# RWKV time mix of a two-layer decoder: logs in place of sigmoid and reciprocal sweeps, and the output product of each chunk placed among the next chunk's products

## The reference

```python
xn = _layernorm(x, ln1_g, ln1_b)
r = jax.nn.sigmoid(jnp.einsum('bsd,ed->bse', xn, Wr))
w = -jnp.exp(jnp.einsum('bsd,ed->bse', xn, Ww))
k = jnp.einsum('bsd,ed->bse', xn, Wk)
v = jnp.einsum('bsd,ed->bse', xn, Wv)
ewk = jnp.exp(w + k)
decay = jnp.exp(time_decay)
def step(carry, inp):          # over the 2048 tokens
    num, den = carry
    e, vt = inp
    num = decay * num + e * vt
    den = decay * den + e
    wkv = num / (den + WKV_EPS)
    return ((num, den), wkv)
...
x = x + jnp.einsum('bsd,ed->bse', r * wkv, Wo)
x = x + _channel_mix(_layernorm(x, ln2_g, ln2_b), Wkey, Wval, Wrec)
```

## Time and profile before

| | |
|---|---|
| median of three runs | 2051.83 us |
| profiled execution | 2051.46 us, span 2049.6 us |
| PE busy | 1775.0 us, 87% of the span |
| DVE busy | 1097.3 us, 54% |
| ACT busy | 962.7 us, 47% |
| POOL busy | 293.1 us, 14% |
| mean granted TensorE clock | 0.936 of full |

### The profile page before, as it was taken

One profiled execution on the slowest core, in us unless ns is written; L12 is line 12 of the kernel. 1 busy time (PEld: TensorE's weight loads), 2 busy tenths in 40 slices (PEclk: granted clock), 3 DMA queues, 4 the chain that ended last, 5 costly groups with the idle time before them and its releaser, 6 DMA issues. The chain is left out here.

```text
span 2049.6 us, 45610 instructions
## 1 busy us (share of the span) xinstructions
PE 1775.0 (87%) x16832; PEld 919.2 (45%) x16833; DVE 1097.3 (54%) x1492; ACT 962.7 (47%) x1695; POOL 293.1 (14%) x306
## 2 busy tenths in 40 slices
PE   6979996999979977684999999999999839999992
PEld 2334432444324423231355545545555326777771
DVE  4553237788331142743888868868878061222224
ACT  3242133777620143423288868868878622222222
POOL 5135010101020020311000000000000112233220
PEclk9989997999989989797899999999999969999996
DMA  6001042110100000417000000000000091001103
GB/s 247 25 34 50 0 68 76 35 34 27 59 1 0 0 5 0 50 22 149 11 10 12 17 11 11 18 11 11 19 3 3 11 385 32 31 31 33 33 28 131
DMA packets 54382, 88.92 MB, mean 43 GB/s; under 512 B 10800, under 2 KB 46576, under 8 KB 52282
## 3 DMA queue, kind: packets, MB, share of 16 engines
q1 hardware_dynamic: 48442, 74.28, 12.7%
q0 software_dynamic: 3648, 9.97, 1.6%
q10 hardware_dynamic: 2112, 2.10, 0.3%
HBM read 65.33 MB, written 20.58 MB: 42 GB/s over the span
## 5 line engine op out<-in xcount | busy, mean ns | idle before, releaser
L1275 ACT ACTIVATE arena<-ps 128x512 f32<-128x512 f32 x1088 | 597.9, 602 | 176.1 <-PE ps L1191 142.5
L1326 DVE TENSOR_REDUCE arena<-ps 128x1 f32<-128x802 f32 (+1 forms) x512 | 493.9, 989 | 76.7 <-PE ps L1123 75.1
L522 PE MATMUL ps<-arena 128*128 (+1 forms) x832 | 374.4, 610 | 57.0 <-DVE arena L1618 22.5
L1123 PE MATMUL ps<-arena 97*32 97x400 bf16 (+2 forms) x5120 | 356.8, 355 | 56.4 <-DVE arena L1326 22.5
L1191 PE MATMUL ps<-arena 100*32 100x512 bf16 x4352 | 389.0, 385 | 11.6 <-issue 7.3
L1166 PE MATMUL ps<-arena 128*32 128x256 f32 x4352 | 333.7, 381 | 2.0 <-ACT arena L1254 1.1
L522 PEld LDWEIGHTS ps<-arena 128*128 128x128 f32 x832 | 161.5, 196 | 268.6 <-issue 262.6
L1123 PEld LDWEIGHTS ps<-arena 97*32 97x32 bf16 x5120 | 130.2, 98 | 211.6 <-DVE arena L1326 69.1
L1806 PE MATMUL ps<-arena 128*128 x608 | 194.9, 463 | 0.8 <-ACT arena L1882 0.8
L1191 PEld LDWEIGHTS ps<-arena 100*32 100x32 bf16 x4352 | 120.5, 98 | 134.4 <-ACT arena L1275 34.3
L1166 PEld LDWEIGHTS ps<-arena 128*32 128x32 f32 x4352 | 135.2, 111 | 101.5 <-issue 9.3
(11 more groups left out here) (209 smaller groups left out, 1463.9 us busy)
## 6 DMA issues: line engine op xcount, KB each, us to landing
arena<-in_experts_w SPq DMA_DIRECT2D x8, 2176.0 KB, 21.2
arena<-qparts SPq DMA_DIRECT2D x192, 64.0 KB, 2.3
qparts<-arena SPq DMA_DIRECT2D x48, 128.0 KB, 2.0
arena<-in_ctxT SPq DMA_DIRECT2D x3, 1664.0 KB, 9.7
kparts<-arena SPq DMA_DIRECT2D x24, 208.0 KB, 2.3
arena<-kparts SPq DMA_DIRECT2D x12, 416.0 KB, 14.2
arena<-rows_out SPq DMA_DIRECT2D x8, 512.0 KB, 7.7
arena<-in_w_rwkv SPq DMA_DIRECT2D x1, 2560.0 KB, 15.3
```

Source lines behind the costliest of these rows:

```text
L522: ins = eng.matmul(out, w[:, k, m * P:(m + 1) * P], x[:, k, tok(c)], start=k == 0, stop=k == ktiles - 1)
L1123: ins = eng.matmul(slot_banks(s_static)[j:j + 32, x, 0:n_keys], Qst[0:97, ring, heads[x], q * P + j:q * P + j + 32], Kst[0:97, at_head(rin ...
L1275: eng.activation(probs[:, keys_of(u, kt) % 2, h, :], ring_bank(r), ACT.Exp, bias=0.0).then_inc(ring_read.sem, 1)
L1326: eng.tensor_reduce(MX[:, par, heads[0] * QT + q, n % 2:n % 2 + 1], got, AX.XY, ALU.max).then_inc(slot_free.sem, 1)
```

## The change

Sigmoid and division are both written with logarithms: ACT takes exp(-r) from PSUM and log(1 + exp(-r)), then log(den); DVE adds the two, and ACT takes the exponential of minus the sum, which is sigmoid(r) / den. All functions come from one table set. The copy of r and one of the two multiplications of DVE go, an addition comes. Everything is done chunk by chunk, with loops written out. The product with Wo of chunk c-1 ("out product") stands between Wk and Wv of chunk c, in banks 0 and 1, and so the products with Wr from chunk 2 on wait for the addition x1 of two chunks before. The last out product stands alone behind the last Wv. The half additions of the normalisation (L427) wait, besides x1, for all scans of num, since they write into B5.

```diff
--- before.py
+++ after.py
@@ -606,45 +606,67 @@
             early_keys[1].store(eng)
 
         mix = stage("mix_products", 4)
-        r_out, w_exp = stage("r_copied", primed="dve"), stage("w_exponential", primed="act")
-        k_sub, k_exp = stage("k_less_w", primed="dve"), stage("k_exponential")
-        v_mul = stage("k_times_v", primed="dve")
-        den_scan, num_scan = stage("den_scanned", 2), stage("num_scanned", 2)
-        r_sig, den_ln, den_inv = stage("r_sigmoid"), stage("den_log"), stage("den_inverse")
-        wkv, r_wkv = stage("wkv"), stage("r_wkv")
+        neg_r_exp, w_exp, k_sub, k_exp = stage("neg_r_exponential"), stage("w_exponential"), stage("k_less_w"), stage("k_exponential")
+        v_mul, den_scan, num_scan = stage("k_times_v"), stage("den_scanned", 2), stage("num_scanned", 2)
+        neg_r_ln, den_ln, logs_added = stage("r_log"), stage("den_log"), stage("logs_added")
+        inverse, r_wkv = stage("r_over_den"), stage("r_wkv")
+        wo, x1 = stage("time_mix_out"), stage("x_plus_time_mix")
 
         @part("pe")
         def _(eng, last=norms[-1]):
             eng.wait_ge(ld_rwkv[0], 16)
             last.wait_all(eng)
             early_keys[1].kept.wait(eng, NC)
-            with eng.Fori(0, NC) as c:
+
+            def mix_product(c, i, w):
+                product(eng, ps[:, 2 * i, :], rwkv[w], 0, XN, c)
+                product(eng, ps[:, 2 * i + 1, :], rwkv[w], 1, XN, c).then_inc(mix.sem, 1)
+
+            def out_product(c):
+                r_wkv.wait(eng, c)
+                product(eng, ps[:, 0, :], rwkv["Wo"], 0, XN, c)
+                product(eng, ps[:, 1, :], rwkv["Wo"], 1, XN, c).then_inc(wo.sem, 1)
+
+            for c in range(NC):
                 ln1.wait(eng, c)
-                for i, (w, read) in enumerate((("Wr", r_out), ("Ww", w_exp), ("Wk", k_sub), ("Wv", v_mul))):
-                    read.wait(eng, c, 0)
-                    product(eng, ps[:, 2 * i, :], rwkv[w], 0, XN, c)
-                    product(eng, ps[:, 2 * i + 1, :], rwkv[w], 1, XN, c).then_inc(mix.sem, 1)
+                if c == 1:
+                    neg_r_exp.wait(eng, 0)
+                if c > 1:
+                    x1.wait(eng, c - 2)
+                mix_product(c, 0, "Wr")
+                if c:
+                    w_exp.wait(eng, c - 1)
+                mix_product(c, 1, "Ww")
+                if c:
+                    k_sub.wait(eng, c - 1)
+                mix_product(c, 2, "Wk")
+                if c:
+                    eng.wait_ge(ld_rwkv[1], 16)
+                    neg_r_exp.wait(eng, c)
+                    out_product(c - 1)
+                    v_mul.wait(eng, c - 1)
+                mix_product(c, 3, "Wv")
+            x1.wait(eng, NC - 2)
+            out_product(NC - 1)
 
         @part("act")
         def _(eng):
-            with eng.Fori(0, NC) as c:
+            for c in range(NC):
+                mix.wait(eng, c, 1)
+                eng.activation(B1[:, :, tok(c)], ps[:, 0:2, :], ACT.Exp, bias=0.0, scale=-1.0).then_inc(neg_r_exp.sem, 1)
                 mix.wait(eng, c, 2)
                 eng.activation(B2[:, :, tok(c)], ps[:, 2:4, :], ACT.Exp, bias=0.0).then_inc(w_exp.sem, 1)
+                neg_r_exp.wait(eng, c)
+                eng.activation(B1[:, :, tok(c)], B1[:, :, tok(c)], ACT.Ln, bias=1.0).then_inc(neg_r_ln.sem, 1)
                 k_sub.wait(eng, c)
                 eng.activation(B3[:, :, tok(c)], B3[:, :, tok(c)], ACT.Exp, bias=0.0).then_inc(k_exp.sem, 1)
-            eng.preload_act_table_set(SIGMOID)
-            with eng.Fori(0, NC) as c:
-                r_out.wait(eng, c)
-                eng.activation(B1[:, :, tok(c)], B1[:, :, tok(c)], ACT.Sigmoid, bias=0.0).then_inc(r_sig.sem, 1)
-            eng.preload_act_table_set(LN_EXP)
-            with eng.Fori(0, NC) as c:
                 den_scan.wait(eng, c)
-                num_scan.wait(eng, c)
-                eng.activation(B3[:, :, tok(c)], B2[:, :, tok(c)], ACT.Ln, bias=WKV_EPS).then_inc(den_ln.sem, 1)
-            den_ln.wait_all(eng)
-            with eng.Fori(0, NC) as c:
-                eng.activation(B3[:, :, tok(c)], B3[:, :, tok(c)], ACT.Exp, bias=0.0,
-                               scale=-1.0).then_inc(den_inv.sem, 1)
+                if c:
+                    logs_added.wait(eng, c - 1)
+                eng.activation(rest, B2[:, :, tok(c)], ACT.Ln, bias=WKV_EPS).then_inc(den_ln.sem, 1)
+                logs_added.wait(eng, c)
+                eng.activation(B1[:, :, tok(c)], B1[:, :, tok(c)], ACT.Exp, bias=0.0,
+                               scale=-1.0).then_inc(inverse.sem, 1)
 
         def scan(eng, st, coef, data, out, h, c, first):
 
@@ -661,54 +683,40 @@
             eng.wait_ge(mask_row_out, 16)
             eng.wait_ge(act_const, 1)
 
-            def mix_and_scan(c, first):
-                mix.wait(eng, c, 1)
-                eng.tensor_copy(B1[:, :, tok(c)], ps[:, 0:2, :]).then_inc(r_out.sem, 1)
+            def add_x(c):
+                wo.wait(eng, c)
+                eng.tensor_tensor(B2[:, :, tok(c)], ps[:, 0:2, :], X[:, :, tok(c)], ALU.add).then_inc(x1.sem, 1)
+
+            for c in range(NC):
                 mix.wait(eng, c, 3)
                 w_exp.wait(eng, c)
                 eng.tensor_tensor(B3[:, :, tok(c)], ps[:, 4:6, :], B2[:, :, tok(c)],
                                   ALU.subtract).then_inc(k_sub.sem, 1)
+                k_exp.wait(eng, c)
+                for h in range(2):
+                    scan(eng, den_scan, decay[:, h:h + 1].broadcast_to([P, CH]), B3, B2, h, c, c == 0)
+                if c:
+                    den_scan.wait(eng, c)
+                    add_x(c - 1)
+                neg_r_ln.wait(eng, c)
+                den_ln.wait(eng, c)
+                eng.tensor_tensor(B1[:, :, tok(c)], B1[:, :, tok(c)], rest, ALU.add).then_inc(logs_added.sem, 1)
                 mix.wait(eng, c, 4)
-                k_exp.wait(eng, c)
                 eng.tensor_tensor(B4[:, :, tok(c)], ps[:, 6:8, :], B3[:, :, tok(c)], ALU.mult).then_inc(v_mul.sem, 1)
                 v_mul.wait(eng, c)
                 for h in range(2):
-                    d = decay[:, h:h + 1].broadcast_to([P, CH])
-                    scan(eng, den_scan, d, B3, B2, h, c, first)
-                    scan(eng, num_scan, d, B4, B5, h, c, first)
-
-            mix_and_scan(0, True)
-            with eng.Fori(1, NC) as c:
-                mix_and_scan(c, False)
-            with eng.Fori(0, NC) as c:
-                den_inv.wait(eng, c)
+                    scan(eng, num_scan, decay[:, h:h + 1].broadcast_to([P, CH]), B4, B5, h, c, c == 0)
                 num_scan.wait(eng, c)
-                eng.tensor_tensor(B4[:, :, tok(c)], B5[:, :, tok(c)], B3[:, :, tok(c)], ALU.mult).then_inc(wkv.sem, 1)
-                wkv.wait(eng, c)
-                r_sig.wait(eng, c)
-                eng.tensor_tensor(XN[:, :, tok(c)], B4[:, :, tok(c)], B1[:, :, tok(c)],
+                inverse.wait(eng, c)
+                eng.tensor_tensor(XN[:, :, tok(c)], B5[:, :, tok(c)], B1[:, :, tok(c)],
                                   ALU.mult).then_inc(r_wkv.sem, 1)
-
-        wo = stage("time_mix_out")
-        x1 = stage("x_plus_time_mix")
-
-        @part("pe")
-        def _(eng):
-            eng.wait_ge(ld_rwkv[1], 16)
-            all_done(r_out, w_exp, k_sub, v_mul)(eng)
-            with eng.Fori(0, NC) as c:
-                r_wkv.wait(eng, c)
-                product(eng, bank(c * 2), rwkv["Wo"], 0, XN, c)
-                product(eng, bank(c * 2 + 1), rwkv["Wo"], 1, XN, c).then_inc(wo.sem, 1)
-
-        @part("dve")
-        def _(eng):
-            with eng.Fori(0, NC) as c:
-                wo.wait(eng, c)
-                eng.tensor_tensor(B2[:, :, tok(c)], bank(c * 2, 2), X[:, :, tok(c)], ALU.add).then_inc(x1.sem, 1)
-
-
-        ln2 = normalise("ln2", B2, ready_of(x1), XN, all_done(x1), vec["ln2_g"], vec["ln2_b"],
+            add_x(NC - 1)
+
+        def x1_ready(eng, c):
+            num_scan.wait_all(eng)
+            x1.wait(eng, c)
+
+        ln2 = normalise("ln2", B2, x1_ready, XN, all_done(x1), vec["ln2_g"], vec["ln2_b"],
                         early=early_keys[1])
 
         @part("sync")
```

## The result

Four runs of the changed kernel have a median of 2035.59 us (2034.17 to 2037.2), beside 2051.85 us for four runs of the kernel before: a ratio of 0.9919, 95% interval 0.9907 to 0.9931. It is 16.3 us faster, where 7.7 were forecast; 2035.59 lies under the range (2040.0 to 2047.6). Two repeats gave 0.9935 (0.9918 to 0.9952) and 0.9931 (0.9917 to 0.9945). Over all 13 runs the median is 2037.45, and over 66 runs of the kernel before 2051.82: 14.4 us.

The account below looks back on a forecast made before the run. The stage was taken as bound by PE at both ends with a serial chain between: 32.02 us go, 24.3 come (10.29 + 0.3 + 6.8 + 5.38 + 1.52), so 2051.46 - 7.7 = 2043.8 us, range 2040.0 to 2047.6.

Parts of the forecast that it names:

- The step that failed: Behind the last addition x1: everything later moves forward by the same amount; the normalisation's own change taken as 0.
- The stage: Time mix up to the last addition x1: ends at 121.7 instead of 129.48 us, 7.7 us less.
- Chain of the last chunk: Serial DVE and ACT steps from k_less_w(3) to the last out product: 13.1 us, 13.4 with POOL.
- PE's waits on x1: Wr of chunks 2 and 3 waits for the addition two chunks before: 0.3 us in all, ends -0.3 and +0.8.
- The handoff from PE to the last addition: Between the last out product's end on PE and its addition on DVE: 0.29 us.
- POOL as neighbour: POOL's half additions beside the last r_wkv slow that DVE product by 0.3 us, ends 0 and 0.6.
- Clock: PE's clock halves about 5 us after its stop; the last out product loses 1.95 us and takes 5.38.
- PE's growth: Three out products inside chunks 1 to 3 put 10.29 us in front of PE's stop.
- The clock held: Rival: no clock fall in PE's 6.8 us stop, last out product takes 3.43 us, time 2041.8 us; chance 0.13.
- the second rival: Clock comes back later: last product wholly at half (+1.5), means partly (+1 to 2), time 2046.6 us; chance 0.15.
- No chunk made PE wait for DVE: Rival: DVE's chain exceeds 17 us, so PE waits before out products; gain used up at 18.1 us; chance 0.05.
- The lower level did not stick: Rival: half clock lasts through means, variances and early key products; 10.8 us slower, 2062 us; chance 0.03.

Follow-up runs that it names:

- e7: Kernel before, with 229 semaphore increments in PE's branch behind the first attention that is not taken: 2048.0 us, ratio 0.9983.
- e9: Kernel before, with 128 semaphore increments in PE's branch behind the first attention that is not taken: 2048.11 us, ratio 0.9981.
- e11: Changed kernel, with 27 semaphore increments in PE's branch behind the first attention that is not taken: 2040.78 us, ratio 0.9942.
- e3: Kernel before, with the nine loops of the time mix and its addition written out, order of work as before: 2047.33 us, ratio 0.9983.
- e2: Changed kernel, with ten idle multiplications on DVE in front of the last addition of x: 2046.95 us, ratio 0.9978.
- e8: Changed kernel, with three idle products on PE in its wait for the last r_wkv: 2035.6 us (one run).
- e1: Changed kernel, with all four out products behind the last Wv and the additions of x behind the last r_wkv: 2031.35 us, ratio 0.9897.
- e5: Kernel before, unchanged, profiled a second time: 2052.33 us (one run).
- e10: Kernel before, with 256 semaphore increments in PE's branch behind the first attention that is not taken: 2052.8 us, ratio 1.0000.

## Why the prediction was wrong

**The step that failed** is the one that carried everything behind the stage over unchanged: "The start of the normalisation governs all that follows", "The normalisation then has the same shape ... I take 0", and so 2051.46 - 7.7. The shape of the normalisation is the same (24.39 us, both times), yet the rest became shorter. Of the 14.4 us between the pooled medians 9.4 lie in the stage; 5.0 lie behind it (6.9 by the first four runs). With the stage's 9.4 alone the time would have been 2042.1, inside the range.

The profiles place what lies behind. From the start of the next block to the mean L443 it takes 421.06 and 419.13 us in the two profiles of the kernel before, and 415.43, 415.08 and 416.24 in the three of the changed kernel: 4.5 less on average. From that mean to the end it takes 1474.67 and 1476.67 against 1471.64, 1478.38 and 1475.11, no more than one kernel scatters by itself. The position of the code behind the jump is worth 3.4 to 4.6 us in the kernel before (e7, e9). In the changed kernel e11 brings the long wait back, but its price there is not resolved. What is left of the 5.0, 0.4 to 1.6 us by these ends, stays open: DVE's and ACT's lists grew too, and no run shifts those alone. That the first four runs lie 1.9 below the pooled median is no effect of the change, since the kernel is the same.

The prediction read every wait of the stage and none behind it. A wait on "issue" of 7.45 us stood in the trace of before, and the longer list of PE could be read from the compiled order.

**The stage** was mis-sized by 1.7 us, 7.7 against 9.4, with the right mechanism:

- *Chain of the last chunk*: 13.4 forecast (with 0.3 for POOL), 12.27 measured (101.58 to 113.85). It was added up from handoffs of 0.13 to 0.29 and own waits of 0.18 to 0.26, read in counted loops. In written-out code they are 0.03 (102.81 to 102.84, 103.90 to 103.93), and DVE to PE 0.15. e3 shows the same in the kernel before: written out, L634 begins 0.03 behind L669 instead of 0.13.
- *PE's waits on x1*: 0.3 forecast, 0 measured. The handoff from PE to the last addition: 0.29 forecast, 0.04 measured (119.57 to 119.61).
- *POOL as neighbour*: 0.3 forecast for r_wkv, which took 1.23 as without POOL. Here it is POOL that got slower, and only in the addition that met r_wkv: 2.01, the two behind it 1.26 and 1.27. r_wkv had begun first, at 112.47 against 112.82. In the row that the forecast rests on, L476 began at 138.65 while POOL's additions were running (134.12 to 139.08), and DVE paid 0.29; in e2, where each keeps meeting the other, both pay. So in these traces the one that begins second pays, and the forecast had the order the wrong way round. The GPSIMD Engine Reference of the Trainium skill (Specifications), drawn on in the prediction, says that both contend; these traces agree.
- *Clock*: 1.95 forecast as lost in the last product, 2.05 measured by e8; at full level the lone product takes 3.67 there, not the forecast 3.43. The fall came 2.75 us after the stop (108.41 to 111.16), not 5; that made no difference, since it was down before the product either way. (The earlier fall that the prediction puts at 24.06 lies at 24.12 by its row of 0.53.)
- *The other terms*: PE's growth (three products, 10.29 us) and the hidden table load, copies and context came as forecast.

**The rivals.** The clock held in e1 and e8, where PE had work, and not in the change itself. It came back 4.1 us into the product, within the forecast 3.2 to 4.6, and in time for the means (3.70); so the second rival did not come either. No chunk made PE wait for DVE. The lower level did not stick. The rivals argued about the stage; the miss came from none of them.

## What to carry to other kernels

Put products that are ready into a wait that is bound to come, not in front of it: the three out products inside the chunks delayed the serial chain by what they would have covered. A handoff read in a register-counted loop is no measure for written-out code. And when an edit changes the length of an engine's list, read the "issue" waits behind every jump in the trace: here skipped instructions alone were worth as much as 4.6 us, so gains of that size need a control that shifts the code by itself.

## What the runs showed of the hardware

The wait behind the jump is 7.2 to 8.0 us in four profiles (before, e5, e10, e11) and at most 4.75 us in the ten others, and adding 256 skipped instructions brings it back to the long value. In the four the instruction queue delivers two packets of 16.4 KB between the last product of the attention and the mean, and the mean begins 1.2 to 1.6 us after the second has landed; in the ten the mean begins before the second packet is under way. e8, whose list is 24 instructions longer than the changed kernel's (45424 against 45400 on the pages), lies between: the first record of the mean runs after the first packet, and PE then stands 1.52 us on issue for the second. Runtime: NRT & Kernel Launch of the Trainium skill (Instruction fetch mechanics) says that instructions are refilled in blocks of 16 KiB, 256 instructions, and that a taken branch whose target lies outside the two pages at hand stalls for a fetch. The packets of 16.4 KB and the period of 256 agree; the size of the stall, and that it varies with the place inside a block, only these runs show.
